# Decoder layer on one core: another order of the first stage's layer-norm, down-projection and latent steps

## The chip, the cores and the metric

The kernel runs on one core of one Trainium2 chip. The metric is the device time of one launch in microseconds; of the kernel before there are three timed runs with a median of 1109.15 us (1106.42 to 1109.94). One more execution was taken with the hardware profiler; its own time is 1110.08 us and the span from its first to its last instruction 1108.3 us. Every row below comes from that execution.

## The reference, cut to what matters

A decoder layer with three parts on x of shape (2, 512, 1024):

```python
x = x + attention(layernorm(x), Wq, Wk_down, Wv_down, Wk_up, Wv_up, Wo)
x = x + fake_quant_matmul(layernorm(x), ctx)
x = x + routed_low_rank_ffn(layernorm(x), A_w, B_w, Wq_w, keys)
```

The change touches only the beginning of the attention. There the kernel computes

```python
h   = (x - mean(x)) / sqrt(var(x) + 1e-5)            # per token
kc  = h @ Wk_down.T ; vc = h @ Wv_down.T             # 8 heads x 32 each
lat = concatenate([kc, vc], per head)                # 512 latents per token
k   = lat[:256] @ Wk_up.T ; v = lat[256:] @ Wv_up.T  # follows directly
```

## The kernel before

All 1024 tokens (two batches of 512) lie in eight tiles `t` of 128 tokens, in `x_sb`. A matrix product is made of three float16 products: each operand is stored as a high part (the value rounded to float16, written by ScalarE) and a low part (value minus high part, written by VectorE), and `split_product` (L1667) issues high x high, high x low and low x high, one matmul line (L1672) for all products of the kernel. So every operand costs one ScalarE step ("hi") and behind it one VectorE step ("lo").

**The first stage, for each tile t:**
- VectorE: `ln1_stats(t)` reads the tile in two halves with two bn_stats (L1196), then one bn_aggr (L1201) and `var_eps` (L1202).
- GpSimd: one power of -0.5 per tile (L677), for which VectorE waits in `ln_rstd` (L1209).
- VectorE: `ln1_rstd(t)`, three small operations (L1210 to L1213) that refine it and one that makes `ln_bias` (L1218).
- ScalarE: `ln1_apply(t)` (L890) writes the normalized tile to `hn`, which is a part of `prob` and has two buffers; for t >= 2 it waits until TensorE has turned tile t-2.
- TensorE: `columns(t)` turns it with eight float32 transposes (L1686) into two PSUM banks. Banks too are shared by t and t-2, so `columns(t)` waits for the low parts of t-2.
- ScalarE `columns_hi(t)` (L871) and VectorE `columns_lo(t)` (L1229) write the two parts of both halves into `h_b`, or for half of the second batch into `b12`, a view of `wo_in`; each step counts `ht_hi` or `ht_lo` up by two per tile.

**The down product.** The four blocks `n` of the down weights (loaded into `down_in`, a view of `o_t`) are split by `down_hi(n)` on ScalarE and `down_lo(n)` on VectorE (both 128x1024) into `wo_sb`. TensorE then makes 16 products (pair, hp), four tile pairs times four weight blocks, each of 24 matmuls of 256 columns. Product (pair, 0) waits for `ht_lo` 4 (pair + 1), that is, for the low parts of both tiles of the pair and of all before; products (0, hp) wait for `wo_lo` hp + 1. Products (0, .) and (1, .) belong to the first batch and fill four PSUM banks; when (1, hp) is done, `latent_hi(0, hp)` (four ScalarE steps of 64x256, L882) and `latent_lo(0, hp)` (four on VectorE, L1240) take the latents out of the bank, and only behind them may product (2, hp) write to it (`gen_read`). Products (2, .) and (3, .) do the same for the second batch.

**What sets the order.** Each engine runs its own instruction list in program order and waits with semaphores; the order is written by hand, so it is the order of the calls in each engine's block. Before, ScalarE runs `down_hi(0)`, `ln1_apply(0)`, `ln1_apply(1)` and then for t = 0 to 7: [`latent_hi(0, 0)` ahead of t = 5, `latent_hi(0, 1..3)` ahead of t = 6], `columns_hi(t)`, `ln1_apply(t+2)`, `down_hi(t+1)` while there is one. VectorE runs the statistics and rstd of tiles 0 and 1, `down_lo(0)`, the statistics of tile 2, and then for each t: [the same latents], `columns_lo(t)`, `ln1_rstd(t+2)`, `down_lo(t+1)`, `ln1_stats(t+3)`. TensorE runs `columns(0)`, `columns(1)` and then, in each pair, one `columns` ahead of product (pair, 0) and one ahead of (pair, 1). SyncE issues the loads at the very start: x tile 0, then x tile n+1 and weight block n in turn, then tiles 5 to 7 and the small inputs.

**Behind the stage** come on TensorE the up products `kv_products(n)` (n = 0 to 6, two for each kind and batch), four plain query products, `kv_products(7)`, and then the attention loop over eight groups; the first use of the second batch waits for all of its latents (`gen_read` 8). GpSimd starts its sums over `h_b` (`part_sums`, L701) when `ht_lo` is 16, and goes on with sum n = 1 when VectorE has split the sums of n = 0, which it does behind `kv_lo(1)`.

Of the kernel before, what the change touches and what calls it, by code (L numbers as in the profile page):

```python
# [14 lines left out]
TT = TOK // P  # L15
# [5 lines left out]
HALF = 512  # L21
# [98 lines left out]
DOWN = 4  # L120
# [90 lines left out]
def decoder_layer(nc, x, ctx_in, wq, wdown, wup, wo, a_w, b_w, router_w, keys, quant, ctx_whole, b_whole, kv_whole, out):  # L211
# [8 lines left out]
    with ctx:  # L220
# [204 lines left out]
        def latent_views(b, hp, half, j):  # L425
# [3 lines left out]
            src = bank[64 * half:64 * half + 64, :].rearrange("p (t i j) -> p i j t", i=4, j=2)[:, :, j, :]  # L429
            at = b * SEQ + 64 * (2 * hp + half)  # L430
            return src, [lat[64 * j:64 * j + 64, part, :, at:at + 64] for part in range(2)]

        def down_heads(t):

            return (0,) if t == 5 else (1, 2, 3)

        block = ctx.enter_context(nc.Block())

# [366 lines left out]
        def _(act):  # L805
# [87 lines left out]
            def down_hi(n):  # L893
                act.wait_ge(down_loaded[n], 16)
                split_hi(wo_sb[:, n, 0, :], down_in[:, n, :], wo_hi, S_W)

            down_hi(0)
            for t in range(2):
                ln1_apply(t)
            for t in range(TT):  # L900
                if t in (5, 6):
                    for hp in down_heads(t):
                        latent_hi(0, hp)
                columns_hi(t)
                if t + 2 < TT:
                    ln1_apply(t + 2)
                if t + 1 < DOWN:
                    down_hi(t + 1)
            def up_split(n):

                act.wait_ge(up_loaded[n % 3], 16 * (n // 3 + 1))
# [267 lines left out]
        def _(dve):  # L1179
# [46 lines left out]
            dve.wait_ge(consts, 6)  # L1226
            nc.vector.tensor_copy(ident_b[:, :], ident[:, :]).then_inc(newton, 1)
            newtons[0] += 1
            def columns_lo(t):  # L1229
                for j in range(2):  # L1230
                    dve.wait_ge(ht_hi, 2 * t + j + 1)
                    hi, lo = (h_block(t // QT, j)[:, part, :, t % QT * P:(t % QT + 1) * P] for part in range(2))
                    split_lo(lo, ps[:, 2 * (t % 2) + j, :].rearrange("p (k n) -> p k n", k=4), hi, ht_lo, S_H)
# [10 lines left out]
                dve.wait_ge(wo_hi, n + 1)  # L1244
                split_lo(wo_sb[:, n, 1, :], down_in[:, n, :], wo_sb[:, n, 0, :], wo_lo, S_W)

            turns = {t: ln1_stats(t) for t in range(2)}
            for t in range(2):
                ln1_rstd(t, turns[t])
            down_lo(0)  # L1250
            turns[2] = ln1_stats(2)
            for t in range(TT):
                if t in (5, 6):
                    for hp in down_heads(t):
                        latent_lo(0, hp)
                columns_lo(t)
                if t + 2 < TT:
                    ln1_rstd(t + 2, turns[t + 2])
                if t + 1 < DOWN:
                    down_lo(t + 1)  # L1260
                if t + 3 < TT:
                    turns[t + 3] = ln1_stats(t + 3)
            def block_split(place, slot, number):

                dve.wait_ge(wq_hi, number)
# [398 lines left out]
        def _(pe):  # L1664
# [27 lines left out]
            for pair in range(PAIRS):  # L1692

                b, part = pair // 2, pair % 2
                at = part * 2 * P
                for hp in range(DOWN):
                    if hp < 2 and 2 * pair + 2 + hp < TT:
                        columns(2 * pair + 2 + hp)
                    if hp == 0:
                        pe.wait_ge(ht_lo, 4 * (pair + 1))  # L1700
                    if pair == 0:
                        pe.wait_ge(wo_lo, hp + 1)
                    if b == 1 and part == 0:

                        pe.wait_ge(gen_read, hp + 1)
                    ins = split_product(ps[:, DOWN_BANK[hp], part * 2 * P:(part + 1) * 2 * P],
                                        [(lambda i, k=k: wo_sb[:, hp, i, k * P:(k + 1) * P],
                                          lambda j, k=k: h_block(b, k // 4)[:, j, k % 4, at:at + 2 * P])
                                         for k in range(KT)])
                    if part == 1:  # L1710
                        ins.then_inc(gen_done, 1)
# [353 lines left out]
```

## Time and profile before

| quantity | value |
|---|---|
| timed runs, median (lowest to highest) | 1109.15 us (1106.42 to 1109.94) |
| profiled execution, its own time | 1110.08 us |
| its span | 1108.3 us |
| TensorE busy | 1064.9 us (96%) |
| VectorE busy | 905.2 us (82%) |
| ScalarE busy | 530.3 us (48%) |
| GpSimd busy | 411.6 us (37%) |
| mean granted TensorE clock | 0.989 of 2.4 GHz |

The span is 1.8 us shorter than the execution's own time, and that time is 0.93 us above the median of the timed runs. Times in the rows are counted from the first instruction. A matmul's shown duration contains its run through the array, so that of matmuls in a row the starts, not the durations, tell the pace. DVE is VectorE, ACT ScalarE, POOL GpSimd, PE TensorE; `[x <-E]` behind a row is the idle time of its engine ahead of it, and what ended it.

### The profile page before, as it was taken

Reading aid. Unit: us, or ns where it says so; the run is one execution under the profiler, and the core shown is the slowest. Engines: PE = TensorE matmul, PEld = TensorE weight load, DVE = VectorE, ACT = ScalarE, POOL = GpSimd, SP = SyncE. Lnnn points to the kernel's source line nnn. Section 1 sums busy time; section 2 is a strip of 40 time slices with the busy share of each in tenths; the row PEclk is TensorE's granted clock in tenths of the full one; section 3 lists DMA queues with packets and bytes.
Section 4 is the critical chain, followed back from the end, with each engine's and each line's share of the span. In section 5 each row is a group of like instructions: output and inputs, shape, how many; then the busy total and the mean of one; then the engine's idle time right before and its main releaser. Section 6 shows DMA issues by size and latency. Waiting matters only on the chain.

```text
span 1108.3 us, 19648 instructions
## 1 busy us (share of the span) xinstructions
PE 1064.9 (96%) x6229; PEld 568.7 (51%) x6236; DVE 905.2 (82%) x1861; ACT 530.3 (48%) x1081; POOL 411.6 (37%) x423
## 2 busy tenths in 40 slices
PE   4999998999999999999999999999999998969998
PEld 3876544555555555555555555555555554434443
DVE  6789578988787978787888888787978798888973
ACT  4646366555454445454544455454545453233420
POOL 2049755534353434343442434353434243000000
PEclk8999999999999999999999999999999999989999
DMA  8016145654544445454545554554445378224442
GB/s 315 1 58 257 77 88 136 164 117 110 139 123 114 106 123 136 110 132 116 139 100 124 132 117 112 132 123 114 106 126 136 83 187 230 101 43 82 102 99 86
DMA packets 229601, 135.74 MB, mean 122 GB/s; under 512 B 200112, under 2 KB 202288, under 8 KB 228656
## 3 DMA queue, kind: packets, MB, share of 16 engines
q1 hardware_dynamic: 229552, 135.11, 48.1%
q8 instruction: 27, 0.44, 0.2%
q14 instruction: 22, 0.18, 0.1%
HBM read 68.23 MB, written 17.83 MB: 78 GB/s over the span
## 4 chain that ended last, share of the span: by engine, by line
PE 85%; DVE 8%; ACT 3%; issue 2%; DMA 1%; POOL 1%; SPq 0%; DVEq 0%; ACTq 0%; POOLq 0%
PE ps L1672 81%; PE ps L1924 2%; ACT prob L1034 1%; DVE wo_sb L1188 1%; DVE h_b L1188 1%; DVE prob L1397 1%; PE ps L1995 1%; DMA wq_sb<-wo_in 1%; DVE prob_t L1188 1%; DMA o_t<-in_wdown 1%; PE ps L1686 0%; ACT prob L890 0%; DVE stats L1196 0%; ACT wo_sb L807 0%; DVE wq_sb L1188 0%
## 5 line engine op out<-in xcount | busy, mean ns | idle before, releaser
L771 POOL TENSOR_SCALAR prob<-prob,row_inv 128x128 f32<-128x128 f32 (+3 forms) x256 | 203.5, 815 | 438.0 <-DVE row_inv L1368 438.0
L1672 PE MATMUL ps<-wo_sb,o_t 128*128 128x512 f16 x1536 | 353.0, 380 | 3.6 <-DVE x_sb L1379 3.6
L1672 PE MATMUL ps<-h_b,wq_sb 128*128 128x512 f16 x1524 | 344.9, 381 | 0.0
L1034 ACT ACTIVATE prob<-prob,neg_max 128x128 f32<-128x128 f32 (+3 forms) x256 | 140.6, 550 | 220.8 <-DVE neg_max L1403 220.8
L1672 PEld LDWEIGHTS ps<-h_b,wq_sb 128*128 128x128 f16 x1524 | 148.4, 98 | 178.2 <-issue 4.4
L1672 PEld LDWEIGHTS ps<-wo_sb,o_t 128*128 128x128 f16 x1536 | 147.6, 98 | 173.1 <-DVE x_sb L1379 6.3
L1379 DVE SCALAR_TENSOR_TENSOR x_sb<-ps,x_sb 128x512 f32<-128x512 f32 x256 | 174.2, 686 | 54.8 <-PE ps L1672 53.9
L1672 PE MATMUL ps<-prob_t,v_sb 128*128 128x128 f16 (+2 forms) x960 | 116.6, 274 | 6.5 <-DMA prob_t<-prob_s 6.5
L1672 PE MATMUL ps<-k_t,q_t 128*128 128x512 f16 (+3 forms) x768 | 114.8, 299 | 0.6 <-DVE neg_max L1403 0.5
L1397 DVE CUSTOM_DVE_ANT_0 prob<-ps,mask 128x512 f32<-128x512 f32 (+3 forms) x256 | 110.3, 484 | 2.3 <-issue 1.6
L1672 PEld LDWEIGHTS ps<-prob_t,v_sb 128*128 128x128 f16 x960 | 83.5, 98 | 36.8 <-DMA prob_t<-prob_s 7.3
L807 ACT ACTIVATE q_t<-q_tmp 128x512 f16<-128x512 f32 x60 | 37.8, 630 | 131.8 <-DVE q_tmp L1355 131.8
L1355 DVE SCALAR_TENSOR_TENSOR q_tmp<-ps,q_tmp 128x512 f32<-128x512 f32 x105 | 72.1, 686 | 29.8 <-PE ps L1672 27.4
L1188 DVE SCALAR_TENSOR_TENSOR prob_s<-prob,prob_s 128x1280 f16<-128x1280 f32 x64 | 95.0, 1484 | 0.1
L807 ACT ACTIVATE prob_s<-prob 128x1280 f16<-128x1280 f32 x64 | 80.6, 1259 | 28.0 <-POOL prob L771 27.3
L1672 PEld LDWEIGHTS ps<-k_t,q_t 128*128 128x128 f16 x768 | 66.9, 98 | 51.7 <-issue 1.0
L1188 DVE SCALAR_TENSOR_TENSOR wq_sb<-wq_in,wq_sb 128x512 f16<-128x512 f32 x94 | 67.5, 732 | 0.5 <-ACT wq_sb L807 0.3
L1188 DVE SCALAR_TENSOR_TENSOR q_t<-q_tmp,q_t 128x512 f16<-128x512 f32 x60 | 61.7, 1049 | 0.7 <-ACT q_t L807 0.7
L1188 DVE SCALAR_TENSOR_TENSOR o_t<-ps,o_t 128x512 f16<-128x512 f32 x64 | 44.3, 692 | 20.1 <-ACT o_t L807 20.1
L801 POOL TENSOR_TENSOR rstd<-var_eps,minus_half 128x1 f32<-128x1 f32 x16 | 8.8, 549 | 139.0 <-DVE var_eps L1202 139.0
L807 ACT ACTIVATE wq_sb<-wq_in 128x512 f16<-128x512 f32 x94 | 56.5, 618 | 3.0 <-POOL wq_in L730 3.0
L1034 ACT ACTIVATION_READ_ACCUMULATOR prob<-prob,neg_max 128x1 f32 x256 | 47.8, 187 | 0.0
(146 smaller groups left out, 1138.4 us busy)
## 6 DMA issues: line engine op xcount, KB each, us to landing
wq_in<-in_wq SPq DMA_DIRECT2D x64, 256.0 KB, 3.5
wo_in<-in_wo SPq DMA_DIRECT2D x32, 512.0 KB, 3.9
side_in<-in_ctx SPq DMA_DIRECT2D x16, 512.0 KB, 4.3
kv_parts<-wo_sb SPq DMA_DIRECT2D x7, 1024.0 KB, 5.0
x_sb<-in_x SPq DMA_DIRECT2D x8, 512.0 KB, 9.2
ctx_quantised<-side_out SPq DMA_DIRECT2D x16, 256.0 KB, 2.9
h_b<-ctx_quantised SPq DMA_DIRECT2D x2, 2048.0 KB, 10.8
out<-x_sb SPq DMA_DIRECT2D x8, 512.0 KB, 2.9
```

Source lines behind the costliest of these rows:

```text
L771: ins = nc.gpsimd.tensor_scalar(at, at, row_inv[:, u % 2, q:q + 1], S_P, ALU.mult, ALU.mult)
L801: nc.gpsimd.tensor_tensor(rstd0[:, k * TT + t:k * TT + t + 1], var_eps[:, k * TT + t:k * TT + t + 1], minus_half[:, :], ALU.pow).then_inc( ...
L807: nc.scalar.activation(dst, src, ACT.Copy, scale=scale).then_inc(signal, 1)
L1034: ins = nc.scalar.activation(at, at, ACT.Exp, bias=neg_max[:, n % 2, q:q + 1], scale=SOFTMAX, accum_out=row_sum[:, n % 2, q:q + 1])
L1188: nc.vector.scalar_tensor_tensor(dst, src, scale, hi, ALU.mult, ALU.subtract).then_inc(signal, 1)
L1355: nc.vector.scalar_tensor_tensor(q_tmp[:, dst, :], ps[:, Q_BANK[product % 2], :], Q_OUT, q_tmp[:, src, :], ALU.mult, ALU.add).then_inc(com ...
L1379: nc.vector.scalar_tensor_tensor(at, ps[:, bank, :], WO_OUT, at, ALU.mult, ALU.add).then_inc(wo_read, 1)
L1397: ins = nc.vector.tensor_tensor_reduce(prob[:, u % 2, at:at + width], ps[:, at // HALF, at % HALF:at % HALF + width], mask[:, SEQ - width: ...
L1672: ins = nc.tensor.matmul(out_, lhs(i), rhs(j), start=start and n == 0, stop=stop and n == 3 * len(pairs) - 1)
L1924: ins = nc.tensor.matmul(ps[:, x_banks(t)[j], :], x_qt[:, t % 2, k * P:(k + 1) * P], ctx_q[:, b, k, j * HALF:(j + 1) * HALF], start=k == 0 ...
L1995: ins = nc.tensor.matmul(ps[0:2 * ROUTER, SMALL_BANK, R_COL:R_COL + P], router_sb[:, k, :, :].rearrange("p a r -> p (a r)"), h3_t[:, t % 2 ...
```

## The change

No operation is added or removed; calls are put in another order on three engines. VectorE's statistics of a tile are cut into two halves (`ln1_half`, and `ln1_end`, which takes the second half and finishes the variance), and other work stands between them. `columns_lo` can be called for one half of a tile. Names, operands and semaphores of the single operations are as before.

```diff
@@ ScalarE
-            down_hi(0)
-            for t in range(2):
-                ln1_apply(t)
-            for t in range(TT):
-                if t in (5, 6):
-                    for hp in down_heads(t):
-                        latent_hi(0, hp)
-                columns_hi(t)
-                if t + 2 < TT:
-                    ln1_apply(t + 2)
-                if t + 1 < DOWN:
-                    down_hi(t + 1)
+            ln1_apply(0)
+            down_hi(0)
+            ln1_apply(1)
+            columns_hi(0)
+            columns_hi(1)
+            down_hi(1)
+            down_hi(2)
+            ln1_apply(2)
+            down_hi(3)
+            columns_hi(2)
+            ln1_apply(3)
+            columns_hi(3)
+            ln1_apply(4)
+            latent_hi(0, 0)
+            ln1_apply(5)
+            columns_hi(4)
+            ln1_apply(6)
+            columns_hi(5)
+            latent_hi(0, 1)
+            latent_hi(0, 2)
+            ln1_apply(7)
+            latent_hi(0, 3)
+            columns_hi(6)
+            columns_hi(7)
@@ VectorE
-            turns = {t: ln1_stats(t) for t in range(2)}
-            for t in range(2):
-                ln1_rstd(t, turns[t])
-            down_lo(0)
-            turns[2] = ln1_stats(2)
-            for t in range(TT):
-                if t in (5, 6):
-                    for hp in down_heads(t):
-                        latent_lo(0, hp)
-                columns_lo(t)
-                if t + 2 < TT:
-                    ln1_rstd(t + 2, turns[t + 2])
-                if t + 1 < DOWN:
-                    down_lo(t + 1)
-                if t + 3 < TT:
-                    turns[t + 3] = ln1_stats(t + 3)
+            def ln1_half(t, j):
+                dve.wait_ge(x_loaded[t], 16)
+                return nc.vector.bn_stats(stats[:, t, j, :], x_sb[:, t, j * HALF:(j + 1) * HALF])
+
+            def ln1_end(t):
+                link(ln1_half(t, 1))
+                return ln_variance(t)
+
+            ln1_half(0, 0)
+            turns = {0: ln1_end(0)}
+            ln1_half(1, 0)
+            ln1_rstd(0, turns[0])
+            turns[1] = ln1_end(1)
+            ln1_rstd(1, turns[1])
+            down_lo(0)
+            ln1_half(2, 0)
+            columns_lo(0)
+            columns_lo(1)
+            down_lo(1)
+            turns[2] = ln1_end(2)
+            ln1_half(3, 0)
+            ln1_rstd(2, turns[2])
+            down_lo(2)
+            turns[3] = ln1_end(3)
+            ln1_half(4, 0)
+            ln1_rstd(3, turns[3])
+            columns_lo(2)
+            down_lo(3)
+            turns[4] = ln1_end(4)
+            columns_lo(3, (0,))
+            ln1_rstd(4, turns[4])
+            columns_lo(3, (1,))
+            turns[5] = ln1_stats(5)
+            ln1_half(6, 0)
+            ln1_rstd(5, turns[5])
+            turns[6] = ln1_end(6)
+            latent_lo(0, 0)
+            ln1_rstd(6, turns[6])
+            columns_lo(4)
+            turns[7] = ln1_stats(7)
+            columns_lo(5)
+            ln1_rstd(7, turns[7])
+            for hp in range(1, DOWN):
+                latent_lo(0, hp)
+            columns_lo(6)
+            columns_lo(7)
@@ TensorE
                 for hp in range(DOWN):
-                    if hp < 2 and 2 * pair + 2 + hp < TT:
-                        columns(2 * pair + 2 + hp)
+                    first = max(0, 2 - pair)
+                    if 0 <= hp - first < 2 and 2 * pair + 2 + hp - first < TT:
+                        columns(2 * pair + 2 + hp - first)
```

On TensorE `columns(2)` and `columns(3)` move from ahead of products (0, 0) and (0, 1) to ahead of (0, 2) and (0, 3); `columns(4)` and `columns(5)` move from ahead of (1, 0) and (1, 1) to ahead of (1, 1) and (1, 2); `columns(6)` and `columns(7)` stay ahead of (2, 0) and (2, 1).

## Rows read from the trace of the kernel before

**Rows 1.** The page, part 1: busy time, share of the span, instructions.

```profile
PE 1064.9 (96%) x6229; PEld 568.7 (51%) x6236; DVE 905.2 (82%) x1861; ACT 530.3 (48%) x1081; POOL 411.6 (37%) x423
```

**Rows 2.** Waits, 0 to 75 us: who waited for whom, total, times, longest.

```profile
ACT prob L890 <- DVE ln_bias L1218: 17.7, 6, 3.9
...
DVE wo_sb L1188 <- ACT wo_sb L807: 7.0, 3, 2.3
```

**Rows 3.** Timeline of TensorE, 0 to 75 us: start, duration, what, count, idle before.

```profile
10.05 3.65 PE L1686 MATMUL ps<-ident,prob 128*128 128x128 f32 x16 [10.05 <-ACT prob L890]
15.44 1.10 PE L1686 MATMUL ps<-ident,prob 128*128 128x128 f32 x8 [1.75 <-ACT prob L890]
20.48 4.58 PE L1672 MATMUL ps<-h_b,wo_sb 128*128 128x256 f16 x24 [3.94 <-DVE h_b L1188]
24.89 1.04 PE L1686 MATMUL ps<-ident,prob 128*128 128x128 f32 x8
25.76 5.40 PE L1672 MATMUL ps<-h_b,wo_sb 128*128 128x256 f16 x48
31.79 2.79 PE L1672 MATMUL ps<-h_b,wo_sb 128*128 128x256 f16 x24 [0.62 <-DVE wo_sb L1188]
...
69.35 1.46 PE L1672 MATMUL ps<-o_t,prob_t 128*128 128x512 f16 x6
...
72.92 1.47 PE L1672 MATMUL ps<-o_t,prob_t 128*128 128x512 f16 x6 [0.77 <-DVE o_t L1240]
```

**Rows 4.** The chain that ended last, 13 to 21 us: start, length, what.

```profile
14.15 1.24 ACT prob L890
15.39 0.96 ACT wo_sb L807
...
16.37 1.23 DVE wo_sb L1188
17.59 1.21 DVE stats L1196 x2
...
19.22 1.20 DVE h_b L1188 x2
```

**Rows 5.** Stretches of TensorE: window, length, busy (count), granted clock, DMA share, GB/s.

```profile
10.00:14.00 4.00, 3.65 (x16) 1.00 1.03 420
...
20.50:24.00 3.50, 3.50 (x17) 0.50 1.00 369
```

**Rows 6.** Timelines of VectorE and GpSimd near 6 us, columns as in rows 3.

```profile
7.41 0.15 DVE L1210 TENSOR_TENSOR rstd<-rstd 128x1 f32<-128x1 f32 x1
...
8.16 0.16 DVE L1210 TENSOR_TENSOR rstd<-rstd 128x1 f32<-128x1 f32 x1
```

```profile
5.96 0.56 POOL L677 TENSOR_TENSOR rstd<-var_eps,minus_half 128x1 f32<-128x1 f32 x1 [2.05 <-DVE var_eps L1202]
```

**Rows 7.** Groups by form, 4 to 72 us: busy, mean ns of one, idle before.

```profile
L1240 DVE SCALAR_TENSOR_TENSOR o_t<-ps,o_t 64x256 f16<-64x256 f32 x31 | 13.1, 422 | 7.0 <-ACT o_t L882 6.5
...
L890 ACT ACTIVATE prob<-x_sb,ln_bias,rstd 128x1024 f32<-128x1024 f32 x8 | 9.8, 1236 | 17.7 <-DVE ln_bias L1218 17.7
...
L1188 DVE SCALAR_TENSOR_TENSOR h_b<-ps,h_b 128x512 f16<-128x512 f32 x12 | 7.9, 683 | 0.2 <-ACT h_b L807 0.2
L807 ACT ACTIVATE h_b<-ps 128x512 f16<-128x512 f32 x12 | 6.8, 588 | 0.4 <-PE ps L1686 0.3
```

**Rows 8.** The down weights' loads, by tile: issues, and time to landing.

```profile
L444 SPq DMA_DIRECT2D o_t<-in_wdown x4: 424/473/788, 1.7 to 4.6; - x4
...
DMA to landing us min/median/max: 6.0/8.4/10.8
```

**Rows 9.** Timelines of GpSimd and TensorE behind the stage, and the whole chain's longest piece.

```profile
83.70 1.47 POOL L701 TENSOR_TENSOR q_tmp<-wo_in,h_b 128x512 f32<-128x512 f16 x1 [14.09 <-DVE h_b L1188]
```

```profile
104.14 1.47 PE L1672 MATMUL ps<-o_t,prob_t 128*128 128x512 f16 x6 [0.67 <-DVE prob_t L1188]
```

```profile
183.00 708.26 PE ps L1672 x3933
```

More of the change, by code:

```diff
@@ L431, in latent_views @@
             return src, [lat[64 * j:64 * j + 64, part, :, at:at + 64] for part in range(2)]
-        def down_heads(t):
-            return (0,) if t == 5 else (1, 2, 3)
         block = ctx.enter_context(nc.Block())
@@ L1228, in _, with columns_lo @@
             newtons[0] += 1
-            def columns_lo(t):
-                for j in range(2):
+            def columns_lo(t, halves=(0, 1)):
+                for j in halves:
                     dve.wait_ge(ht_hi, 2 * t + j + 1)
```

## The prediction

> **What bounds the kernel now.** I read the page first: TensorE is busy for 96% of the span [rows 1], so only time in which it stands still or runs slowly can be won, unless work is taken away, and none is. The list of waits and TensorE's timeline of the first 75 us then show where it stands still: nothing runs before 10.05, 1.75 us pass ahead of tile 2's transposes, 3.94 us ahead of the first down product, 0.62 us ahead of the third, 0.77 us ahead of the third up product; from 31.79 to the up products it never stops [rows 3]. So the stage has two halves. Until 20.48 TensorE waits for other engines, and behind that it is the bound itself. What another order can win is the start of product (0, 0), plus the gap at 31.79.
>
> Why is that start so late? The chain of waits answers it [rows 4]. Both tiles of pair 0 were turned by 13.7, but between them and the last low parts VectorE did other work: it waited for ScalarE's high part of weight block 1, which ScalarE had put behind normalizing tile 2 (14.15 to 16.3), then took that block's low part (16.37) and the statistics of tile 3 (17.59), and only then tile 1's low parts (19.22). The same pattern gives VectorE its 7.0 us of waits for weight high parts in 3 waits, and ScalarE 17.7 us for `ln_bias` [rows 2]: each tile's work went round the engines as a ring.
>
> **The change, part by part.**
>
> 1. *Start of tile 0.* The power on GpSimd for tile 0 lies at 5.96 and takes 0.56, to 6.52. VectorE used it only at 7.41, behind both statistics and the variance of tile 1 [rows 6]. Now only one half's statistics (0.6, half of 1.21 [rows 4]) stand there, so `ln1_rstd(0)` starts at about 6.6. Its four small operations take 0.75, the step from 7.41 to 8.16, where tile 1's begin [rows 6], and `ln1_apply(0)` can start at 7.45 and end at 8.7 (1.24 each [rows 7]). It now stands ahead of `down_hi(0)`, whose load lands at 1.7 + 6.0 = 7.7 anyway [rows 8], so TensorE's first transposes start at about 8.7, not 10.05.
>
> 2. *Tile 1.* The second half, the variance and the power (0.7 with its link, then 0.42, the time from 18.80 to 19.22 in the chain [rows 4], then 0.6; behind 7.35) are exposed now: `ln1_rstd(1)` starts at 9.2 and ends at 10.0. On ScalarE `down_hi(0)` (8.6 to 9.65) fills that time. `ln1_apply(1)` runs from 10.0 to 11.25, and tile 1's transposes take half of the 3.65 us that 16 needed [rows 3], rounded up to 1.95: 11.3 to 13.25. That is 0.45 us earlier than before.
>
> 3. *Low parts of the pair.* ScalarE's last high part follows at 13.3 (0.59 [rows 7]), VectorE's at 13.9 (0.68 [rows 7]). VectorE has nothing between: `down_lo(0)` ends at 11.1 and one half of tile 2's statistics at 11.8. **Product (0, 0) starts at 14.65 in place of 20.48: 5.83 us earlier.** This is the main term.
>
> 4. *TensorE's own work behind it.* Tile 2's eight transposes used to be done in the dead time; now they lie behind product (0, 1), in the dense part: +0.87 us, the step from 24.89 to 25.76 [rows 3]. Tiles 3 to 7 were in the dense part already, so they cost nothing new.
>
> 5. *The gap at 31.79.* The two products from 25.76 take 2 x 2.62 us (2.62 is what a product takes when dense: from 31.79 to 69.35 there are 13 products and 4 tiles' transposes, and (37.56 - 4 x 0.87) / 13 = 2.62), so they end their issue at 31.0 and the gap is worth 0.79 [rows 3]. With the new order weight block 3 reaches VectorE in time (next paragraph): -0.79.
>
> The sum is 5.83 - 0.87 + 0.79 = **5.75 us**, if the first product runs at the same pace as now.
>
> **Is the rest of the list early enough?** TensorE's needs from 14.65 follow by adding: (0, 1) at 19.05, tile 2 at 21.7, (0, 2) at 22.55, tile 3 at 25.2, (0, 3) at 26.05, (1, 0) at 28.65, (1, 1) at 32.15, tile 5 at 34.8, (2, 0) at 41.75, (3, 0) at 53.1. Against them I walk VectorE and ScalarE through their new lists, with 0.60 for a low part behind another, 1.14 to 1.23 for a weight's, 1.21 for two statistics [rows 4], 1.7 for four latents (4 x 0.422 [rows 7]), 0.96 for a weight's high part [rows 4]. Low part of block 1: 14.9 to 16.1, 2.9 us early. Block 2: the four loads land between 7.7 and 15.4 [rows 8], evenly spaced (an estimate) the third at 12.8; ScalarE takes it at 14.75, VectorE at 18.6 to 19.8, 2.7 early. Block 3: landed at 4.6 + 10.8 = 15.4, ScalarE at 19.85, VectorE at 24.0 to 25.25, 0.8 early. Tile 3's last low part: 28.4, which is 0.25 early, the tightest point. Tile 5's normalizing stands behind `latent_hi(0, 0)`, which waits for product (1, 0) at 31.45: 1.56 + 1.24 gives 34.3, 0.5 early. Tile 7's stands behind `latent_hi(0, 2)` and ends at 42.1, 2.2 early. VectorE's last `latent_lo(0, 3)` ends at 45.7 for (2, 3) at 50.5, and tile 7's low parts, which now stand behind three blocks of latents, end at 48.2 for (3, 0) at 53.1, 4.9 early. What hides each edit is therefore TensorE's products; if the cover were gone, each late item costs its own lateness once, not its length.
>
> **Behind the stage** the times hang together. The third up product waited 0.77 us for the latents of (3, 3) [rows 3], and will again. Between 83 and 104 VectorE is the bound and TensorE waits for it (0.67 us at 104.14); GpSimd's second sum starts at 83.70 on a VectorE step [rows 9]. Both chains start from TensorE's own up products or from VectorE steps that follow them, so they move with it. GpSimd's first sum starts with the last low part, at 48.2, and there were 14.09 us idle behind it [rows 9], so it is not late. From 183.00 the chain is 708 us of TensorE alone [rows 9]. I see nothing there that is fixed in absolute time, so the 5.75 us reach the end whole.
>
> **The clock** decides the rest. Product (0, 0) took 4.41 us (20.48 to 24.89) at a granted 0.50, that is 1.2 GHz, against 2.62 dense [rows 3, 5]: 1.79 us lost. TensorE had stood still for 3.94 us before. Now only 1.4 us pass before it. Of the first transposes 16 took 3.65, 0.23 each, the next eight 1.10, 0.14 each, and later eight have 0.87 between starts [rows 3]. The view of stretches shows 1.00 for 10 to 14 [rows 5], but the pace is half, so I take it that the clock was low there and rose at the end of those 16. If it rises as early this time, product (0, 0) saves up to 1.79, but then VectorE's list is the bound (tile 3's low part is only 0.25 early, then later latents shift by less), and walking it again with a fast first product I get 0.75 more: **6.5 us**. If the rise comes later, into product (0, 1), up to 1.2 us of it is lost too: **4.55 us**. I keep the same 4.41, since that is the row I have, and both ends for the range.
>
> The Trainium skill ("TensorE: Matmul & The Clock Gate", Part 4: PE-mode transpose) says that a transpose does not count as busy for the clock gate. By that rule transposes alone would never raise the clock and the 4.41 would be sure, so the gain would be 5.75 at most. The float32 transposes of this trace do not agree, 0.23 us each first and 0.14 then.
>
> A measurement of this kernel can tell about 0.3% (3.3 us) from no change.
>
> **The rivals.**
> - *The clock comes late or early*, 4.55 or 6.5 us. For it: only 1.4 us of rest before the product, but a pause of 0.6 between the tiles too. These are ends of the forecast, not another sign.
> - *Part of it is given back* (chance 0.09). If my walk of VectorE is a few tenths short at each of the tight points (0.25, 0.5 and 0.8 us of cover) and the stretch from 83 to 104, where VectorE has no rest, does not move with TensorE, the gain shrinks. Against it: that VectorE stretch begins with high parts of up products. Worked out: 5.75 less 2 us of lateness and 1.7 us of present TensorE waits that would grow to twice that leaves 2.1 us: 1107.1 us, within the bound.
> - *It is slower* (0.03): the clock. If TensorE stays at 1.2 GHz in the down products, every us at it loses half a us. To eat 5.75 and add 3.3 more, it must stay there 18 us longer than the 3.6 us of the row, through (1, 1); 1112.5 us or more. Against it: 3.6 us of products raised it [rows 3, 5], and TensorE does not rest any more after 14.65.
> - *It does not do what it says* (part of the 0.09): if tile 1's normalizing were held up by `down_hi(0)` because its load came late. At 7.7 [rows 8] there is 0.9 to spare.
>
> **The numbers.** Profiled execution: 1110.08 - 5.75 = 1104.3. Against the median, which is 0.93 lower, 1109.15 - 5.75 = 1103.4. The range runs from 6.5 us and some 1.5 us of scatter of a median (1101.2) to 4.55 us and 1.2 of scatter (1105.8). Chances: forecast with its two ends 0.88, faster by more than 0.3%; 0.09 within it; 0.03 slower.
>
> **What would show it.** In the changed profile: transposes from 8.7 and 11.3, product (0, 0) at 14.6 to 14.7, no idle time of TensorE from there to the up products, no wait of VectorE for a weight's high part over 0.5 us, third up product at 67.2 (66.4 to 68.4), first wait behind it again for `o_t`. Wrong would be a start of (0, 0) behind 16, new gaps of TensorE at (0, 3), (1, 0) or tile 5, or a third up product at 67 with an end that did not move.

## The result, and the profile after

The changed kernel takes **1102.91 us** (median of four runs, 1102.20 to 1103.88) against 1109.55 us for the kernel before (four runs). The ratio is 0.9948 with a 95% interval of 0.9932 to 0.9965, that is 5.8 us less, between 3.9 and 7.5 (the two medians differ by 6.6). The forecast was 1103.4 us with a range of 1101.2 to 1105.8, and a chance of 0.88 that the kernel is faster. The profiled execution took 1102.57 us with a span of 1100.8.

First TensorE's timeline of the changed kernel (columns as in [rows 3], whose lines these answer to):

```profile
8.68 1.94 PE L1724 MATMUL ps<-ident,prob 128*128 128x128 f32 x8 [8.68 <-ACT prob L886]
11.08 1.97 PE L1724 MATMUL ps<-ident,prob 128*128 128x128 f32 x8 [0.46 <-ACT prob L886]
14.46 5.41 PE L1710 MATMUL ps<-h_b,wo_sb 128*128 128x256 f16 x48 [1.41 <-DVE h_b L1196]
19.78 1.09 PE L1724 MATMUL ps<-ident,prob 128*128 128x128 f32 x8
20.71 2.78 PE L1710 MATMUL ps<-h_b,wo_sb 128*128 128x256 f16 x24
23.40 1.09 PE L1724 MATMUL ps<-ident,prob 128*128 128x128 f32 x8
24.40 2.79 PE L1710 MATMUL ps<-h_b,wo_sb 128*128 128x256 f16 x24
27.50 2.79 PE L1710 MATMUL ps<-h_b,wo_sb 128*128 128x256 f16 x24 [0.30 <-DVE h_b L1196]
...
66.00 1.47 PE L1710 MATMUL ps<-o_t,prob_t 128*128 128x512 f16 x6 [0.77 <-DVE o_t L1248]
```

Three things are to be seen. Product (0, 0) starts at 14.46 (forecast 14.65), and 48 matmuls take 5.41 us, the full pace: there is no slow first product. TensorE then has one marked gap, 0.30 us ahead of product (1, 0) at 27.50, for VectorE's low parts. And the third up product starts at **66.00** against 72.92 [rows 3], **6.92 us** earlier (forecast 5.75, with 6.5 at the full clock).

The waits of the changed kernel, 0 to 75 us, show what became of the two lines of [rows 2]:

```profile
ACT prob L886 <- DVE ln_bias L1226: 11.0, 6, 5.3
...
DVE wo_sb L1196 <- ACT wo_sb L803: 2.2, 4, 0.6
```

VectorE's waits for weight high parts fell from 7.0 to 2.2 us, the longest from 2.3 to 0.6. Of the four waits that are left only one, of 0.25 us at 14.66, lies ahead of 27.5. The chain that ended last (start, length, what) now runs through VectorE's list up to 27.5 and then through TensorE alone:

```profile
14.66 1.22 DVE wo_sb L1196
15.88 0.61 DVE stats L1257
17.00 0.56 POOL rstd L673
18.38 1.14 DVE wo_sb L1196
19.52 0.61 DVE stats L1257
20.63 0.56 POOL rstd L673
22.01 1.20 DVE h_b L1196 x2
23.21 1.13 DVE wo_sb L1196
24.34 0.61 DVE stats L1257
25.46 0.56 POOL rstd L673
26.84 0.61 DVE h_b L1196
27.50 2.79 PE ps L1710 x24
```

Pieces of 0.22 us and less between these lines are left out. GpSimd's pieces of 0.56 us cost VectorE nothing: its timeline has other work beside each of them (one half's statistics or one half's low part) and no wait from 15.8 to 27.5. Before, the same stretch of the chain went ScalarE, ScalarE, VectorE, VectorE, VectorE for every tile [rows 4]; now ScalarE is not on it any more.

**Behind the stage** the shift is still 6.92 us at the product that started at 104.14 [rows 9] and now starts at 97.22. Further on, short spells of low clock take from it and give back. Two pairs of TensorE's lines show this. Before:

```profile
183.00 1.81 PE L1672 MATMUL ps<-prob_t,v_sb 128*128 128x128 f16 x15 [2.07 <-DMA prob_t<-prob_s]
...
927.68 7.04 PE L1672 MATMUL ps<-wo_sb,o_t 128*128 128x512 f16 x24 [2.42 <-DVE x_sb L1379]
```

After:

```profile
176.61 3.24 PE L1710 MATMUL ps<-prob_t,v_sb 128*128 128x128 f16 x15 [2.28 <-DMA prob_t<-prob_s]
...
922.93 5.35 PE L1710 MATMUL ps<-wo_sb,o_t 128*128 128x512 f16 x24 [2.41 <-DVE x_sb L1417]
```

The view of stretches (window, length, busy, granted clock, DMA share, GB/s) has the spells. Before:

```profile
170.00:176.00 6.00, 5.36 (x25) 0.72 0.43 134
176.00:182.00 6.00, 4.93 (x28) 1.00 0.51 96
925.00:930.00 5.00, 2.58 (x10) 0.87 0.98 326
```

After:

```profile
170.00:176.00 6.00, 4.32 (x24) 1.00 0.63 113
176.00:182.00 6.00, 5.39 (x25) 0.72 0.45 119
925.00:930.00 5.00, 5.00 (x30) 1.00 0.99 246
```

Between 140 and 165 the shift falls from 6.9 to 6.4 us, in a stretch where TensorE waits for transfers; why is open. The spell near 173 in the kernel before lies ahead of one more wait for a transfer (up to 183.00) and costs nothing: the shift is 6.4 us on either side of it. The one near 178 in the changed kernel lies behind that wait and costs 1.7 us: the shift falls from 6.39 us to 4.73 by 190, and is 4.75 at 922.93. There only the kernel before has a spell, which gives 1.69 us back: TensorE's 111 matmuls of the end of the attention start at 932.08 in place of 938.51 (-6.43). A last difference of this kind lies near 995 (a granted clock of 0.68 from 990 to 1000 before, 0.87 after), and the span is 7.5 us shorter. That the two profiles end so near to the stage's 6.92 is therefore this pair's luck, as the repeated run below shows.

### The profile page after: what moved, and what is told of

Its sections match the earlier page's. It is cut to its first block, busy times and chain, and to the rows that moved or that the text cites. A ratio compares the mean times of both kernels' runs of the same rounds, so it can differ in the third digit from the quotient of the medians.

```text
span 1100.8 us, 19648 instructions
## 1 busy us (share of the span) xinstructions
PE 1061.0 (96%) x6229; PEld 565.9 (51%) x6236; DVE 905.5 (82%) x1861; ACT 530.6 (48%) x1081; POOL 410.9 (37%) x423
## 4 chain that ended last, share of the span: by engine, by line
PE 85%; DVE 8%; ACT 3%; issue 2%; POOL 1%; DMA 1%; POOLq 0%; DVEq 0%; ACTq 0%; SPq 0%
PE ps L1710 82%; PE ps L1963 2%; ACT prob L1042 1%; DVE wo_sb L1196 1%; DVE prob L1435 1%; DVE h_b L1196 1%; PE ps L2034 1%; DMA wq_sb<-wo_in 1%; DVE prob_t L1196 1%; PE ps L1724 0%; DVE stats L1257 0%; DVE wq_sb L1196 0%; DVE o_t L1196 0%; DMA prob_t<-prob_s 0%; POOL prob L767 0%
## 5 line engine op out<-in xcount | busy, mean ns | idle before, releaser
L803 ACT ACTIVATE prob_s<-prob 128x1280 f16<-128x1280 f32 x64 | 80.6, 1259 | 28.4 <-POOL prob L767 27.3
```

Source lines behind the costliest of these rows:

```text
L803: nc.scalar.activation(dst, src, ACT.Copy, scale=scale).then_inc(signal, 1)
```

## The experiments

All edits are against the changed kernel, except two against the kernel before. The measure is the start of the third up product in the profile (66.00 with the change, 72.92 without), because a time tells apart 2 us at best. "Pace" is the shown duration of the first 48 down matmuls, products (0, 0) and (0, 1): 5.4 us at the full clock. Behind each time stands its ratio to the kernel before with the 95% interval. The edited kernels were timed in three sets, in which the kernel before had medians of 1108.06, 1109.18 and 1108.11 us; so compare the ratios, not the medians.

| kernel | (0, 0) starts | pace | third up product | median us | ratio |
|---|---|---|---|---|---|
| before (profile) | 20.48 | (0, 0) alone: 4.4 | 72.92 | 1109.55 | |
| changed | 14.46 | 5.41 | 66.00 | 1102.91 | 0.9948 (0.9932 to 0.9965) |
| changed, again | 14.30 | 5.42 | 65.85 | 1103.22 | 0.9952 (0.9936 to 0.9968) |
| TensorE's order old | 21.53 | | 76.89 | 1113.45 | 1.0054 (1.0033 to 1.0074) |
| before + TensorE's order new | 20.72 | 7.33 | 77.98 | 1113.13 | 1.0042 (1.0029 to 1.0054) |
| tile 1's low parts late | 16.51 | 7.46 | 69.29 | 1105.49 | 0.9972 (0.9960 to 0.9983) |
| weight high parts late | 14.49 | 7.12 | 70.85 | 1107.41 | 0.9983 (0.9968 to 0.9999) |
| old start | 15.37 | 7.23 | 67.93 | 1104.01 | 0.9956 (0.9935 to 0.9977) |
| latents late | 14.23 | 5.41 | 65.77 | 1102.90 | 0.9940 (0.9921 to 0.9960) |
| before + transposes in the rest | 21.76 | full | 72.89 | 1109.91 | 1.0009 (0.9996 to 1.0023) |
| 72 products ahead | 14.63 | 5.42 | 65.85 | 1101.03 | 0.9937 (0.9915 to 0.9958) |
| VectorE relieved | 14.48 | 6.77 | 66.95 | 1103.46 | 0.9952 (0.9938 to 0.9966) |
| both | 14.60 | 5.41 | 65.75 | 1101.93 | 0.9931 (0.9916 to 0.9946) |
| both, 44 products | 14.09 | 5.41 | 65.23 | 1101.75 | 0.9946 (0.9933 to 0.9960) |

### One engine's order alone

TensorE's old order in the changed kernel:

```diff
-                    first = max(0, 2 - pair)
-                    if 0 <= hp - first < 2 and 2 * pair + 2 + hp - first < TT:
-                        columns(2 * pair + 2 + hp - first)
+                    if hp < 2 and 2 * pair + 2 + hp < TT:
+                        columns(2 * pair + 2 + hp)
```

> The changed kernel with TensorE's list alone put back: the transposes of tiles 2 and 3 stand again ahead of products (0, 0) and (0, 1), those of 4 and 5 ahead of (1, 0) and (1, 1). Theory: tile 2 is normalized at 18.5 to 19.7 in the new order of ScalarE, so product (0, 0) starts behind its transposes at about 20.6, TensorE rests for 7 us before it, and the whole gain of the stage is lost: third up product at 72 to 74 (66.0 with the change, 72.9 without), time as of the kernel before or up to 1.5 us more. Rival (the orders of ScalarE and VectorE bring the gain by themselves): third up product at 67 to 68, time within 2 us of the changed kernel.

The theory had the direction, but not the size: 76.89 and 6 us over the kernel before. Its timeline of TensorE, two lines:

```profile
19.77 1.97 PE L1724 MATMUL ps<-ident,prob 128*128 128x128 f32 x8 [6.73 <-ACT prob L886]
...
40.21 1.97 PE L1724 MATMUL ps<-ident,prob 128*128 128x128 f32 x8 [2.91 <-ACT prob L886]
```

The 6.73 us of rest were foreseen. The second gap was not: with the old order tile 5's transposes stand ahead of product (1, 1), while ScalarE normalizes tile 5 only behind `latent_hi(0, 0)`, which waits for product (1, 0). Behind it the clock was low again (72 matmuls in 8.80 us in place of 8.02); without the 2.91 and the 0.78 us it would be 73.2, within the 72 to 74 expected. By this trace the latents' new place needs TensorE's new order; no run tested the two apart.

The same hunk the other way round, as the only edit to the kernel before:

> The kernel before with only TensorE's new order. Theory: VectorE still reaches tile 1's last low part at 19.8 to 20.4, so product (0, 0) starts at 20.5 as before and tile 2's transposes, no longer done in the dead time, are added behind (0, 1), and ScalarE and VectorE, whose lists expect tile 2 early, are late with block 3: third up product at 73.5 to 78 (72.9 before), time 1 to 5 us above the kernel before. Rival: the new order alone gives the gain: third up product near 67.

77.98 and 4.7 us more, as the theory said. Two lines of TensorE's timeline:

```profile
20.72 7.33 PE L1672 MATMUL ps<-h_b,wo_sb 128*128 128x256 f16 x48 [6.78 <-DVE h_b L1188]
...
34.74 7.08 PE L1672 MATMUL ps<-h_b,wo_sb 128*128 128x256 f16 x48 [2.32 <-DVE wo_sb L1188]
```

The start is the old one (20.72), and now weight block 3 comes 2.3 us late, because the ring of tiles and weights starts tile 2 later. The clock has its part too: the 48 matmuls from 34.74 took 7.08 us, at the full clock they take 5.40. **Neither half of the change is worth anything alone; TensorE's costs 4.7 us, the other two engines' 6.0, and together they give 5.8.**

### What in the new lists counts

Tile 1's low parts back behind weight block 1 and tile 2's statistics:

```diff
@@ ScalarE
-            columns_hi(1)
             down_hi(1)
+            columns_hi(1)
@@ VectorE
-            columns_lo(1)
             down_lo(1)
             turns[2] = ln1_end(2)
+            columns_lo(1)
```

> The changed kernel with only tile 1's low parts put back behind the low part of weight block 1 and the end of tile 2's statistics (and ScalarE's high parts of tile 1 behind weight block 1's). Theory: product (0, 0) starts at 16.3 to 16.8 in place of 14.46, and as TensorE has hardly a gap behind it, nearly all of it counts: third up product at 67.4 to 68 with the full clock in product (0, 0), 69 to 69.6 with the low one, for the longer rest makes it likelier. Rival (VectorE's list up to tile 3 is what counts, and its sum is unchanged): third up product at 66.0 to 66.5.

Product (0, 0) started at 16.51 as expected, and the clock was low:

```profile
16.51 7.46 PE L1710 MATMUL ps<-h_b,wo_sb 128*128 128x256 f16 x48 [3.44 <-DVE h_b L1196]
```

69.29 can be added up: the start is 2.05 later, the pace costs 2.05 (7.46 less 5.41), and the slack that the changed kernel has from 14.46 to 27.50 is used up. That slack is 0.82: five pieces from 14.46 without a pause (5.24 + 0.87 + 2.62 + 0.87 + 2.62) would end at 26.68, and (1, 0) starts at 27.50. 66.00 + 2.05 + 2.05 - 0.82 = 69.28. So the rival, that only VectorE's sum counts, falls: the order of the low parts counts as well. Of the 3.29 us, 1.23 are the later start (2.05 less the slack) and 2.05 the clock of this execution.

High parts of weight blocks 2 and 3 back behind the normalizing of tiles 2 and 3:

```diff
             down_hi(1)
-            down_hi(2)
             ln1_apply(2)
-            down_hi(3)
+            down_hi(2)
             columns_hi(2)
             ln1_apply(3)
+            down_hi(3)
```

> The changed kernel with ScalarE's high parts of weight blocks 2 and 3 behind the normalizing of tiles 2 and 3, as in the old ring. Theory (VectorE's list up to tile 3 is the bound, and it was slow because it waited for these): VectorE waits about 2.3 us for block 2, tile 3's last low part ends near 30 in place of 27.4, TensorE has a gap of 1.5 to 2.5 us ahead of (0, 2) or (1, 0), third up product at 67.8 to 69, whatever the clock in product (0, 0). Rival (only the start of product (0, 0) counts): third up product at 66.0 to 67.4.

Here (0, 0) started in time, at 14.49, and yet 4.85 us were lost. VectorE's and then TensorE's timelines:

```profile
20.73 1.23 DVE L1196 SCALAR_TENSOR_TENSOR wo_sb<-o_t,wo_sb 128x1024 f16<-128x1024 f32 x1 [2.33 <-ACT wo_sb L803]
```

```profile
25.84 1.09 PE L1724 MATMUL ps<-ident,prob 128*128 128x128 f32 x8 [0.74 <-ACT prob L886]
28.05 7.08 PE L1710 MATMUL ps<-h_b,wo_sb 128*128 128x256 f16 x48 [1.12 <-DVE wo_sb L1196]
```

VectorE's wait is the expected 2.3, and the rival falls. But 70.85 lies outside the 67.8 to 69 expected. The gaps lie elsewhere than I wrote, ahead of tile 3 and of (0, 3), and I had left out their second price: (0, 3) and (1, 0) took 7.08 in place of 5.40, as the clock was low again behind these short rests (granted 0.57 from 28 to 32). (1, 0) starts at 28.05 + 2.62 = 30.67 by the full pace, 3.17 late, and 1.68 more from the pace are the 4.85. Two weight high parts, one and two places further down on ScalarE's list, take back two thirds of the change's gain in this trace, and of its gain in time (1.9 us by the ratio are left of 5.8). Without the clock's 1.68 us it is 3.17 of 6.92.

The old start (both statistics of tiles 0 and 1 ahead of both rstd, weight block 0 first on ScalarE):

```diff
@@ ScalarE
-            ln1_apply(0)
             down_hi(0)
+            ln1_apply(0)
             ln1_apply(1)
@@ VectorE
-            ln1_half(0, 0)
-            turns = {0: ln1_end(0)}
-            ln1_half(1, 0)
-            ln1_rstd(0, turns[0])
-            turns[1] = ln1_end(1)
-            ln1_rstd(1, turns[1])
+            turns = {t: ln1_stats(t) for t in range(2)}
+            for t in range(2):
+                ln1_rstd(t, turns[t])
```

> The changed kernel with the start as before: both statistics of tiles 0 and 1 on VectorE ahead of both rstd, and the first weight block's high part ahead of tile 0's normalizing. Theory: transposes from 10.0 to 13.7 without a pause, last low part of tile 1 at 15.0, product (0, 0) at 15.1 in place of 14.46; VectorE's list behind it moves by the same 0.6, and product (1, 0) starts at 28.1: third up product at 66.4 to 66.8 (66.0 with the change). Rival (the start decides most of the gain): third up product later than 68.

67.93, outside of what I expected, though by the clock: start 0.91 later, pace 1.82 slower, less the 0.82 of slack gives 1.91, and 1.93 were measured. The start itself is worth 0.1 us behind that slack. Whether the new start also helps to have the full clock in the first product is left open: with it the clock was full in some executions and low in others (the last section).

The latents back in their old places:

```diff
@@ ScalarE
             ln1_apply(4)
-            latent_hi(0, 0)
             ln1_apply(5)
             columns_hi(4)
             ln1_apply(6)
+            latent_hi(0, 0)
             columns_hi(5)
-            latent_hi(0, 1)
-            latent_hi(0, 2)
             ln1_apply(7)
+            latent_hi(0, 1)
+            latent_hi(0, 2)
             latent_hi(0, 3)
@@ VectorE
-            latent_lo(0, 0)
             ln1_rstd(6, turns[6])
             columns_lo(4)
             turns[7] = ln1_stats(7)
+            latent_lo(0, 0)
             columns_lo(5)
```

> The changed kernel with the latents of the first batch where the old lists have them: (0, 0) behind tile 6's normalizing and ahead of tile 5's parts, (0, 1) to (0, 3) together behind tile 7's normalizing. Theory (TensorE's products cover all of it, 2 to 5 us each): third up product at 66.0 as with the change, or 67.0 to 67.8 if the clock is low in product (0, 0); TensorE without a gap from (1, 0) to the up products; time within 0.1% of the changed kernel. Rival (the latents' place is part of the gain): a gap ahead of product (2, 0) or of one behind it, of 0.5 us or more.

65.77, and TensorE had no gap behind (1, 0): the latents' place is worth nothing, TensorE's products cover it either way.

### The clock

The kernel before, with 32 transposes of a constant in TensorE's rest ahead of product (0, 0):

```diff
+            def filler(count):
+                for _ in range(count):
+                    nc.tensor.transpose(ps[:, 7, 0:P], ident[:, :], ident[:, :])
...
                     if hp < 2 and 2 * pair + 2 + hp < TT:
                         columns(2 * pair + 2 + hp)
+                    if pair == 0 and hp == 0:
+                        filler(32)
```

> The kernel before with 32 more float32 transposes of a constant behind those of tile 2, into a PSUM bank that is free then: about 3.5 us of TensorE work in the 3.94 us in which it waits for product (0, 0). Theory (the clock fell because TensorE rested, and float32 transposes keep it up): granted clock 1.00 throughout, product (0, 0) in 2.6 in place of 4.4 us, third up product at 71.1 to 71.6 (72.9 before; the 1.79 us, less what the third product then waits longer for its weights, as VectorE's list does not move). Rival (transposes do not count as work for the clock): 4.4 us and 72.9 as before.

The clock part came true and the gain did not. TensorE's timeline:

```profile
15.42 1.97 PE L1686 MATMUL ps<-ident,prob 128*128 128x128 f32 x8 [1.75 <-ACT prob L890]
17.18 4.74 PE L1693 MATMUL ps<-ident 128*128 128x128 f32 x32
21.76 2.78 PE L1672 MATMUL ps<-h_b,wo_sb 128*128 128x256 f16 x24
...
31.76 2.79 PE L1672 MATMUL ps<-h_b,wo_sb 128*128 128x256 f16 x24 [1.10 <-DVE wo_sb L1188]
```

Its stretches (columns as above), two of them:

```profile
17.00:18.00 1.00, 1.00 (x6) 1.00 1.02 406
...
20.00:21.00 1.00, 1.00 (x12) 1.00 1.10 343
```

The transposes went from 6 to 12 in a us, and product (0, 0) took 2.8; having started 1.28 us later than before, it ended half a us earlier. But product (0, 3) started at 31.76, as before (31.79 [rows 3]): it waits for VectorE's low part of weight block 3, whose list did not move. The gap ahead of it grew from 0.62 to 1.10 us instead. **The 1.79 us of low clock in the kernel before had cost nothing.** VectorE's list was the bound up to 31.7.

Here the trace does not agree with the Trainium skill ("TensorE: Matmul & The Clock Gate", Part 4: PE-mode transpose), by which a transpose does not count as work for the clock. Nothing but float32 transposes ran from 15.42 to 21.76, and the pace doubled in the middle of them.

### Can the rest be had?

Four versions that leave the reference's computation as it is. Ahead of TensorE's list, products of a constant:

```diff
+            for _ in range(72):
+                nc.tensor.matmul(ps[:, 7, 0:P], ones[:, :], ones[:, :], start=True, stop=True)
             for t in range(2):
                 columns(t)
```

> The changed kernel with 72 float16 products of a constant at the start of TensorE's list, into a PSUM bank that is free then. They begin when the constants are there (about 3.9) and take 72 x 0.055 to 0.11 us, so they run while TensorE would wait for tile 0 (8.7). Theory: the first transposes then run at the full clock, 0.87 in place of 1.95 us for a tile, tile 1's from 11.1 to 12.0, product (0, 0) at 13.4 in place of 14.46. But VectorE's list is the bound at tile 3's last low part (27.4 with the change), and the earlier start reaches it in small part only: the gaps ahead of product (1, 0) grow to 1 us or more, third up product at 65.3 to 65.9 (66.0). Rival (TensorE's start is the bound): third up product at 64.9 or less. Time: within 0.1% of the changed kernel by the theory.

They took 7.0 us and ended at 10.8, past the 8.7 at which tile 0 was ready, so tile 0's transposes were late, though both tiles' then took 1.9 us together in place of 3.9. (0, 0) started at 14.63, not at 13.4, and (1, 0) again when VectorE let it:

```profile
27.34 2.79 PE L1710 MATMUL ps<-h_b,wo_sb 128*128 128x256 f16 x24 [0.30 <-DVE h_b L1196]
```

VectorE relieved of a part of tile 4's work ahead of tile 3's last low part:

```diff
-            ln1_half(4, 0)
             ln1_rstd(3, turns[3])
             columns_lo(2)
             down_lo(3)
-            turns[4] = ln1_end(4)
-            columns_lo(3, (0,))
-            ln1_rstd(4, turns[4])
-            columns_lo(3, (1,))
-            turns[5] = ln1_stats(5)
+            ln1_half(4, 0)
+            columns_lo(3)
+            turns[4] = ln1_end(4)
+            ln1_half(5, 0)
+            ln1_rstd(4, turns[4])
+            turns[5] = ln1_end(5)
```

> The changed kernel with VectorE's half of tile 4's statistics, its end and its rstd moved behind tile 3's last low part (2.4 us of VectorE work, less the power's wait that they hid). Theory: VectorE ends tile 3's low parts at 25.5 to 26.5 in place of 27.4, so product (1, 0) starts at 27.2 without a gap and the third up product at 65.6 to 65.7, if TensorE keeps the full clock in product (0, 0); if the clock is low there, at 67.2 to 67.4. Tile 4 is normalized by 29.9, when its transposes are due. Rival (tile 4 is late): a new gap ahead of its transposes and no gain.

The edit moves less than the expectation says: the first half of tile 4's statistics still stands ahead of tile 3's low parts, and only the second half, the variance and `ln1_rstd(4)` go behind them. The gap ahead of (1, 0) is gone all the same, one of 0.16 us ahead of tile 4's transposes has come (the rival's part of it), and the pace of this execution was 6.77, between my two cases; 66.95 is what these give.

Both edits together:

> Both edits together: 72 products of a constant ahead of TensorE's list, and tile 4's statistics behind tile 3's last low part. Theory (with VectorE's list relieved, the earlier start of TensorE counts): product (0, 0) at 13.4, third up product at 64.6 to 65.1 in place of 66.0, that is 1 us or so, 0.1% of the time, hardly to be told by the times. Rival (another VectorE or ScalarE step, such as weight block 3 or tile 5, ends last then): third up product as in the better of the two single edits.

65.75, a miss: with 72 products the start was 14.60 and not 13.4. So the same once more with 44 products:

> As the run with both edits, with 44 in place of 72 products of a constant, so that they end at about 8.6, when tile 0 is ready, and not at 10.8. Theory (TensorE's start counts once VectorE's list up to tile 3 is relieved): transposes from 8.7 at the full pace, product (0, 0) at 13.2 to 13.6, third up product at 64.4 to 65.1 (66.0 with the change, 65.75 with 72 products). Rival (VectorE's other steps, the two weight blocks and tile 3's power, still end last): gaps of TensorE ahead of (0, 3), tile 3 or (1, 0) and a third up product at 65.4 to 65.8.

```profile
3.96 4.73 PE L1729 MATMUL ps<-ones 128*128 128x128 f16 x44 [3.96 <-POOL mask L669]
8.59 1.09 PE L1724 MATMUL ps<-ident,prob 128*128 128x128 f32 x8
11.09 1.09 PE L1724 MATMUL ps<-ident,prob 128*128 128x128 f32 x8 [1.41 <-ACT prob L886]
14.09 5.41 PE L1710 MATMUL ps<-h_b,wo_sb 128*128 128x256 f16 x48 [1.91 <-DVE h_b L1196]
```

65.23, the earliest of all and just outside my 64.4 to 65.1. The transposes are fast, but (0, 0) starts at 14.09 for VectorE's low parts, whose timeline leaves no pause between the first of them and the low part of weight block 1:

```profile
11.55 2.48 DVE L1196 SCALAR_TENSOR_TENSOR h_b<-ps,h_b 128x512 f16<-128x512 f32 x4
13.95 1.23 DVE L1196 SCALAR_TENSOR_TENSOR wo_sb<-o_t,wo_sb 128x1024 f16<-128x1024 f32 x1
```

What the four versions still win over the changed kernel is 0.8 us at most by the trace (66.00 less 65.23). The times can't tell these versions from the changed kernel (ratios 0.9931 to 0.9952, each give or take 0.0013 to 0.0022): all of them beat the kernel before and none is shown to beat the changed one.

### The changed kernel again

> The changed kernel once more, to see how far the clock in product (0, 0) and behind the stage is a matter of the single execution. Theory: product (0, 0) starts at 14.4 to 14.7 again; products (0, 0) and (0, 1) take 5.4 to 7.3 us together; third up product between 66.0 and 67.4, by that pace alone; the time 5 to 7.5 us below the kernel before. Rival (the full clock there belongs to this order): 5.4 us and 66.0 again.

65.85 and the full pace; the execution's span was 1103.5 against 1100.8, although its third up product was no later. It has the spell near 177 as the first profile has it, and near 925 also that of the kernel before:

```profile
922.81 7.04 PE L1710 MATMUL ps<-wo_sb,o_t 128*128 128x512 f16 x24 [2.42 <-DVE x_sb L1417]
```

So 7.07 us won in the stage were 4.8 us of span in this execution. The interval from the third up product to the end is 1034.8 in the changed kernel's first profile, 1037.7 in this one, 1035.4 in that of before, and 1031.6 to 1037.3 in the others.

One profile can't tell, then, whether the stage's gain reaches the end; all runs together can. Over the 13 rows of the table that have a ratio, the time won (1 less the ratio, times the median of the kernel before) rises with the shift of the third up product by 1.00 us per us (standard error 0.06), at 0.7 us less on average. The clock's luck does not make the gain either: among executions with the same mean granted clock, the medians are 1110.28 before and 1103.40 after at 0.992 (ten and five), 1108.0 and 1102.4 at 0.995 (fifteen and two), so 6.9 and 5.6 us apart. **What the stage wins is carried to the end on average, under a scatter of some 3 us to either side in single executions.**

## Why the prediction was right, and where its steps were not

*The bound.* Right that TensorE waited for other engines first and was the bound then. Wrong in where the line lies: I put it at 20.48, the start of (0, 0), and it was at 31.79, where product (0, 3) waited for weight block 3. (The text calls this product the third; it is the fourth.) The transposes put into the rest show it: a fast first product moved nothing behind 31.8.

*The sum.* Its terms 5.83, -0.87 and +0.79 measured 6.02 (20.48 to 14.46), -0.87 and +0.79. It compares the path through TensorE before with that after, at the same pace of the first product and with no pause of TensorE behind 14.65. Two terms stood at nothing there and did not measure nothing: +1.79 for the pace of the first product and -0.82 for the pauses up to 27.50. 6.02 - 0.87 + 0.79 + 1.79 - 0.82 = 6.91. The true difference is simpler: (1, 0) started at 35.29 before (31.79, then 2.62 for (0, 3) and 0.87 for tile 4's transposes), and at 27.50 after; 7.79, less tile 4's transposes (0.87), which now stand behind it, is 6.92, what the third up product shows.

*The clock* is the term that was mis-sized. I kept 4.41 us for the first product and gave 5.75; in three profiles with this start the product was fast, the gain 6.92 to 7.15, and the end that I had given for it, 6.5, was 0.4 to 0.65 short, about what I had VectorE later than it was. I had also called the loss of 1.79 us a cost of the kernel before, and it was none. With the slow pace the stage gave 4.99 (old start, 67.93) and 5.97 (VectorE relieved, 66.95), so the two ends were the right idea.

*The lateness of the rest.* The walk held: weight high parts waited for 0.6 us at most, tile 3's last low part was the tightest (forecast 28.4, measured 27.45), and (2, 3) and (3, 0) never waited. But not tile 5 came next, with its half us of cover: with the fast first product tile 2, tile 3 and weight block 3 were ready at 19.72, 23.35 and 24.34, only about 0.05 us ahead of the starts at 19.78, 23.40 and 24.40, and TensorE lost about a tenth at each. The walk has small slips that cost nothing: its own terms put `ln1_rstd(1)` at 9.07, not 9.2 (measured 8.96), and the 14.15 to 16.3 named as normalizing tile 2 are that (to 15.39) and the weight's high part. The latents' place proved to be covered, as said.

*The way to the end.* That nothing is fixed in absolute time is borne out by the times: a slope of 1.00 over the 13 rows. That the gain would reach the end whole holds on average only; in the first profile it was down to 4.75 us on the way, and in the repeated one it ended at 4.8.

*The rivals.* The part given back did not occur: the waits of TensorE in the up products were 0.37, 0.68 and 0.67 us before and 0.36, 0.67 and 0.67 after. TensorE's stay at the low clock did not occur in the change, but a low clock in products (0, 0) and (0, 1) did in five of the edited kernels, at 1.4 to 2 us each (pace less 5.41), so its price was right and its length far too great.

That the median came out within 0.5 us of the forecast is partly luck: the stage gave 1.2 us more than forecast, and the times (5.8, in the repeated run 5.3) less than the stage. Their intervals hold both.

## What to carry to other kernels

When several engines pass tiles round in a ring, find the step that a waiting engine needs next and look what its supplier does first: here weight high parts ahead of normalizings, and one tile's low parts ahead of the next tile's statistics, were the parts whose undoing cost most (4.85 and 3.29 us of 6.92, clock included; the two are not a sum). What the interleaved halves of the statistics are worth was tested only for the start, where it is 0.1 us; for tiles 2 to 6 it is open. Change the lists of all engines together: here the new order on TensorE alone made the kernel slower by 4.7 us, and that on the other two alone by 6.0. And before a slow stretch of an engine is counted as a loss, look for the next wait behind it on the same engine: if another engine's list ends that wait, the slow stretch was free.

## What the runs showed of the hardware that was not expected

- The same instructions up to 14.5 us gave products (0, 0) and (0, 1) in 5.41, 5.42 and 5.41 us (changed, again, latents late), but 6.77 (VectorE relieved) and 7.12 (weights late), behind much the same rest of 1.41 to 1.50. The clock there differs between single executions. With TensorE at work from 3.96 on (three runs) it was always 5.41 or 5.42, behind a rest of 1.9.
- The granted clock in the records is 1.00 from the start until the first change in them. In the run with tile 1's low parts late the pace of (0, 0) was half of the full one, with this line:

```profile
14.00:20.00 6.00, 3.49 (x17) 1.00 1.02 390
```

  17 recorded matmuls of 256 columns lie in the 3.49 us, about 0.2 each, where the full pace is 0.109 (2.62 for 24). Near the start the pace has to be read from the matmuls.
- Rests of 0.7 and 1.1 us near one another (weights late) were followed by 48 matmuls in 7.08 in place of 5.40 us, at a granted 0.57 from 28 to 32.
- A spell of low clock costs or not by where it falls: near 173, ahead of TensorE's wait for a transfer, it cost nothing, and behind that wait 1.7 us (15 matmuls in 3.24 us in place of 1.81, and 24 more in 5.62 in place of 5.34). Of the fourteen profiles eleven have it behind the wait; three have not, that of the kernel before among them.
